# A quantum-attention tower on one core: 82 later weight pieces split during the second layers instead of where they are used

## The reference

```
for t in (er, ei):  h = gelu(ln(x @ W1.T + b1) * g + be)      # first layer,  2048 -> 2048
                    s_t = (h @ W2.T + b2).reshape(tokens, 4, 512)  # second layer, 2048 -> 4*512
q, k, v (real, imaginary) = s_r, s_i times six 512x512 matrices; attention of 4 states, 8 heads
attn_r, attn_i = out @ Wo.T                                   # two more 512x512
R, I   = per state n: attn_r, attn_i times int_Wr[n], int_Wi[n]    # eight 512x512
sup    = sum_ij cos(phase_i - phase_j) * strength_ij * (R_j, I_j), then normalised
amp    = |sup times meas_M (complex)|;  z = gelu(ln(amp @ post_W.T))
y      = relu(relu([z, r_x] @ W_top1) @ W_top2) @ W_top3
```

## Time and profile before

| what | us |
|---|---|
| runs | 3175.32, 3175.93 (median), 3177.78 |
| the profiled execution: its time / its span | 3182.69 / 3181.0 |
| PE busy, DVE busy, ACT busy | 2999.9 (94%), 1573.5 (49%), 1111.3 (35%) |
| first layers, second layers, states (from the span's start) | 0 to 813, 813 to 1597, 1597 to 3181 |
| mean granted clock of PE | 0.979 |

### The profile page before, as it was taken

One profiled execution on the slowest core, in us unless ns is written; L12 is line 12 of the kernel. 1 busy time (PEld: TensorE's weight loads), 2 busy tenths in 40 slices (PEclk: granted clock), 3 DMA queues, 4 the chain that ended last, 5 costly groups with the idle time before them and its releaser, 6 DMA issues. The chain is left out here.

```text
span 3181.0 us, 43948 instructions
## 1 busy us (share of the span) xinstructions
PE 2999.9 (94%) x15808; PEld 2577.4 (81%) x15808; DVE 1573.5 (49%) x2819; ACT 1111.3 (35%) x1873; POOL 232.9 (7%) x241
## 2 busy tenths in 40 slices
PE   7999999999699999999969999999999989999798
PEld 6888888888588877888859999999999977777686
DVE  3222222112531125212156766767757768999973
ACT  3111111111331114211145555555545564555553
POOL 1000000000110011111000000000000000112000
PEclk9999999999899999999989999999999999999899
DMA  5222222121442334332252232232232274444410
GB/s 196 73 76 73 73 75 73 57 65 63 149 143 75 99 96 136 106 99 84 71 185 54 56 90 66 66 86 59 66 92 53 80 189 89 99 88 96 142 41 11
DMA packets 364352, 285.48 MB, mean 90 GB/s; under 512 B 280192, under 2 KB 280320, under 8 KB 364160
## 3 DMA queue, kind: packets, MB, share of 16 engines
q1 hardware_dynamic: 341632, 206.97, 24.3%
q0 software_dynamic: 22656, 77.67, 7.1%
HBM read 194.40 MB, written 90.18 MB: 89 GB/s over the span
## 5 line engine op out<-in xcount | busy, mean ns | idle before, releaser
L50 PE MATMUL banks<-a_whi,a_xhi 128*128 128x512 f32 x1152 | 450.4, 391 | 24.1 <-DVE a_wlo L179 17.6
L51 PE MATMUL banks<-a_wlo,a_xhi 128*128 128x512 f32 x1152 | 449.4, 390 | 0.0
L52 PE MATMUL banks<-a_whi,a_xlo 128*128 128x512 f32 x1152 | 449.3, 390 | 0.0
L50 PE MATMUL banks<-b_ghi,b_whi 128*128 128x512 f32 x1024 | 402.1, 393 | 10.2 <-DVE b_slo L389 8.6
L52 PE MATMUL banks<-b_ghi,b_wlo 128*128 128x512 f32 x1024 | 399.1, 390 | 0.0
L51 PE MATMUL banks<-b_glo,b_whi 128*128 128x512 f32 x1024 | 399.0, 390 | 0.0
L179 DVE TENSOR_TENSOR a_wlo<-a_wraw,a_whi 128x512 fp32r<-128x512 f32 x144 | 99.7, 693 | 577.6 <-ACT a_whi L165 577.6
L165 ACT ACTIVATE a_whi<-a_wraw 128x512 fp32r<-128x512 f32 x144 | 90.9, 631 | 668.1 <-PE banks L52 629.3
L50 PE MATMUL banks<-t_sx,s_whi 128*128 128x256 f32 x1024 | 292.8, 286 | 28.6 <-DVE s_wlo L1267 24.5
L374 DVE TENSOR_TENSOR b_wlo<-b_wraw,b_whi 128x512 fp32r<-128x512 f32 x128 | 88.3, 691 | 444.8 <-ACT b_whi L326 444.6
L52 PE MATMUL banks<-t_sx,s_wlo 128*128 128x256 f32 x1024 | 289.9, 283 | 0.0
(11 more groups left out here) (156 smaller groups left out, 5562.9 us busy)
## 6 DMA issues: line engine op xcount, KB each, us to landing
a_wraw<-w_first SPq DMA_DIRECT2D x144, 256.0 KB, 2.6
b_wraw<-w_second SPq DMA_DIRECT2D x128, 256.0 KB, 2.6
t_sx<-s_scr SPq DMA_DIRECT2D x64, 512.0 KB, 4.5
a_scr<-t_at SPq DMA_DIRECT2D x256, 128.0 KB, 2.1
s_axng<-a_scr SPq DMA_DIRECT2D x64, 512.0 KB, 5.6
s_wraw<-w_pieces SPq DMA_DIRECT2D x82, 256.0 KB, 4.7
h_scr<-a_hst POOLq DMA_DIRECT2D x72, 256.0 KB, 2.7
b_hl<-h_scr POOLq DMA_DIRECT2D x16, 1024.0 KB, 6.0
```

What stands on the lines that cost most here:

```text
L50: mm(out, ahi, bhi, start=first, stop=False)
L51: mm(out, ahi, blo, start=False, stop=False)
L52: return mm(out, alo, bhi, start=False, stop=last)
```

## The change

All 82 pieces are split once, during the second layers, in chunks 1 to 6 of either branch (6 a chunk), chunk 7 of the first (4) and chunk 0 of the second (6): SP loads a piece into `praw`, ACT and DVE split it into `pnew` after the ring's own pieces of steps 3 to 7, SP stores both halves (512 KB) to `w_scr` in DRAM. The split operands of all phases now share two tensors, `g.hi` and `g.lo`. Where the states need weights, SP loads a group of four pieces as two DMAs of 1 MB (hi and lo) straight into places that have died. The first 8 groups are loaded at the end of the second layers: group q once step q of the last chunk has freed its place. `pieces` is gone from ACT and DVE, and PE waits on `w_in[q]` instead of `w_split`.

```diff
+        PRE = 6
+        def prepared(br, c, x):
+            return br * 46 + c * PRE + (x - PRE)
+        def extra(br, c):
+            return 4 if (br, c) == (0, CH - 1) else PRE if (br, c) == (1, 0) else 0
+        AFTER = {3: (0, 1), 4: (2,), 5: (3,), 6: (4,), 7: (5,)}
...
+            def pre_load(p, x):
+                sp.wait_ge(p_split, p + 1)
+                sp.dma_start(praw[:, x % 2, :], g.w_pieces[p]).then_inc(p_loaded[x % 2], 16)
+            def pre_store(p, x):
+                sp.wait_ge(p_split, p + 3)
+                sp.dma_start(g.w_scr[bass.ds(p, 1)].rearrange("o p h w -> p (o h) w"),
+                             pnew[:, x % 2, :, :].bitcast(F32)).then_inc(p_stored[x % 2], 16)
+            def chunk(br, c, n):
                 for j in range(ST):
...
+                    ring(br * CH + c, j)
+                    if j < min(n, 2):
+                        pre_load(prepared(br, c, j), j)
+                    for x in AFTER.get(j - 1, ()) + ((5,) if j == ST - 1 else ()):
+                        if x < n:
+                            pre_store(prepared(br, c, x), x)
+                        if x + 2 < n:
+                            pre_load(prepared(br, c, x + 2), x + 2)
...
+            for q in range(ST):
+                sp.wait_ge(w_used, (2 * CH - 1) * ST + (SPL + q + 1))
+                g.load_pieces(sp, q, q)
...
+            def pre_high(p, x):
+                act.wait_ge(p_loaded[x % 2], (p - x) * 8 + (16 * (x // 2) + 16))
+                act.wait_ge(p_stored[x % 2], (p - x) * 8 + (16 * (x // 2) + 16))
+                act.activation(pnew[:, x % 2, 0, :], praw[:, x % 2, :], ACT.Copy).then_inc(p_hi, 1)
...
                     for j in range(AHEAD, ST):
                         w_high(br * CH + c, j)
+                        for x in AFTER[j]:
+                            pre_high(prepared(br, c, x), x)
...
@@ phase_states, SP @@
             load_s(0, 0)
             load_s(0, 1)
-            for i in range(NP):
-                piece(i)
...
             sp.wait_ge(projected, LAST_B * 8 + 8)
-            for i in range(NP, NP + 2 * KD):
-                piece(i)
+            for q in range(4):
+                g.load_pieces(sp, q, 8 + q)
             sp.wait_ge(v_full, LAST_B * 4 + 4)
             load(0, 0)
+            for q in range(4, 6):
+                g.load_pieces(sp, q, 8 + q)
             store_a(LAST_B - 1)
             load(0, 1)
-            for i in range(NP + 2 * KD, NP + 4 * KD):
-                piece(i)
             store_a(LAST_B)
-            for i in range(NP + 4 * KD, NP + 6 * KD):
-                piece(i)
+            for q in range(6, 8):
+                g.load_pieces(sp, q, 8 + q)
             load(0, 2)
...
             for n in range(3):
                 load(LAST, n)
-            for i in range(2 * NP, 2 * NP + 2 * KD):
-                piece(i)
+            sp.wait_ge(multiplied, LAST * 8 + 2)
+            g.load_pieces(sp, 0, 16)
+            g.load_pieces(sp, 1, 17)
             load(LAST, 3)
...
+        def load_pieces(eng, q, group):
+            n = min(KD, NPIECE - group * KD)
+            for h, to in enumerate((g.hi, g.lo)):
+                eng.dma_start(to[:, q * KD:q * KD + n, :].bitcast(F32),
+                              g.w_scr[group * KD:group * KD + n, :, h, :].rearrange("i p w -> p i w")).then_inc(g.w_in[q], 16)
```

More of the change, by code:

```diff
@@ L245, in phase_second_layers @@
     with s.ctx:
-        ghi = s.sb("ghi", [P, KI, TOK], F32R)
-        glo = s.sb("glo", [P, KI, TOK], F32R)
+        ghi, glo = (t[:, :, :].rearrange("p (k a) w -> p k (a w)", a=2) for t in (g.hi, g.lo))
         wraw = s.sb("wraw", [P, RAW, W])
@@ L262, in phase_second_layers @@
         w_loaded = [s.sem(f"w_loaded{i}") for i in range(RAW)]
+        p_loaded = [s.sem(f"p_loaded{i}") for i in range(2)]
+        p_stored = [s.sem(f"p_stored{i}") for i in range(2)]
+        p_hi = s.sem("p_hi")
+        p_split = s.sem("p_split")
         w_hi = s.sem("w_hi")
@@ L340, in gain_shift @@
                 return g.cols[:, i:i + 1]
+            for i in range(2):
+                act.sem_inc(p_stored[i], 16)
             act.wait_ge(mv_done, 2 * TT)
@@ L423, in _ @@
                                           ALU.subtract).then_inc(g_split, 1)
+                    for x in AFTER.get(j, ()):
+                        if x < extra(br, 0):
+                            pre_low(prepared(br, 0, x), x)
                 for j in range(AHEAD):
@@ L429, in _ @@
                         w_low(br * CH + c, j)
+                        for x in AFTER[j]:
+                            pre_low(prepared(br, c, x), x)
                     for j in range(AHEAD):
@@ L436, in _ @@
                     w_low(br * CH + (CH - 1), j)
+                    for x in AFTER[j]:
+                        if x < extra(br, CH - 1):
+                            pre_low(prepared(br, CH - 1, x), x)
                 s_low(br, CH - 1)
@@ L514, in phase_states @@
     with s.ctx:
[L515 to L519, removed]
+        whi, wlo = g.hi, g.lo
         ids = s.sb("ids", [P, TT, N], mybir.dt.int32)
@@ L830, in _ @@
             sup_back(2)
-            for i in range(2 * NP + 4 * KD, 2 * NP + N_TOP):
-                piece(i)
             store(LAST - 1)
@@ L935, in t_high @@
                                    bias=bcol(M_O + e, m)).then_inc(t_hi, 1)
-            def pieces(i0, i1):
-                for i in range(i0, i1):
-                    act.wait_ge(w_loaded[i % TR], 16 * (i // TR + 1))
-                    act.activation(whi[:, i % NP, :], wraw[:, i % NP, :], ACT.Copy).then_inc(w_hi, 1)
             def block_body(b, first):
@@ L950, in block_body @@
                         o_high(b - 1, m - 1)
-                    if first and m == 1:
-                        pieces(M_V * KD, M_O * KD)
-                    if first and m == 3:
-                        pieces(M_O * KD, NP)
                 if not first:
@@ L1106, in _ @@
             pt_evac(LAST_B, 0)
-            pieces(NP, NP + 2)
             t_high(LAST_B - 1, 2)
@@ L1117, in _ @@
             o_high(LAST_B, 3)
-            pieces(NP + 4, NP + 2 * KD)
             negate(0, 0)
@@ L1262, in t_low @@
                     ins.then_inc(t_split, 1)
-            def pieces(i0, i1):
-                for i in range(i0, i1):
-                    dve.wait_ge(w_hi, i + 1)
-                    dve.tensor_tensor(wlo[:, i % NP, :], wraw[:, i % NP, :], f32(whi[:, i % NP, :]),
-                                      ALU.subtract).then_inc(w_split, 1)
             def block_body(b, first):
@@ L1513, in _ @@
             tile.units()
-            pieces(2 * NP, 2 * NP + 2 * KD)
             sup_low(0)
@@ L1712, in vectors @@
                             w = (2 * n + (x if part == 0 else 1 - x)) * KD + k
-                            if part == 0 and first:
-                                pe.wait_ge(w_split, NP + w + 1)
+                            if part == 0 and first and k == 0:
+                                pe.wait_ge(g.w_in[2 * n + x], 64)
                             a = ax[:, n % 2, :, k, :]
```

84 lines of the change are left out of this document (42 added, 42 removed).

## The result

| kernel | median, us (lowest to highest, executions) | ratio to before, 95% interval |
|---|---|---|
| before, beside it | 3175.62 (3175.15 to 3177.78, 4) | |
| changed | 3214.24 (3211.89 to 3218.88, 4) | 1.0118 [1.0103, 1.0133] |

A forecast was written before the change was run, and what follows sets the result against it. PE, busy 94% of the span, was taken as the bound, with about 40 us at stake at most. -5.9 + 6.8 + 11.3 - 8.3 = +3.9 on a median of 3175.93 gave 3180 us, range 3166 to 3190.

The forecast's parts named there:

- First layers: same instructions at other addresses, 0: First layers: their instructions are unchanged and only tensor addresses move, so 0 us.
- (a): Start of the states: splitting gone, group loads' queue next in line, PE starts at 1615.1 instead of 1621.05; -5.9 us.
- (b): Second layers, second branch's second chunk: late ring piece +4.5, low clock 1.6, h load +0.7; +6.8 us, bounds 0 and +10.
- (c): End of the blocks: block 14's stores queue behind group loads and hold up ACT, then PE; +11.3 us, bounds -2.7 and +17.
- (d): Last stretch: DVE on the path loses 11.1 us of pieces, PE gains part; -8.3 us, bounds -4.9 and -11.1.
- stores not held back: Rival at the end of the blocks: group loads don't delay stores, -2.7 instead of +11.3, 3166 us; chance 0.15.
- second layers hide all: Rival in the second layers: SP's late ring pieces make no stall, 3180 - 6.8 = 3173 us; chance 0.15.
- groups slower than 345 GB/s: Rival, last chunk and end of blocks: group loads slower than the pieces; at 320 GB/s +10.7, 3191 us; chance 0.22.

The follow-up runs named there:

- e1: Kernel before, with only the split x and split activations of the first two stages moved 320 bytes up by unused memory: 3205.31 us, 1.0088.
- e9: Kernel before, with the operands of its last two stages put at multiples of 256 bytes by pads: 3176.31 us, 0.9998.
- e7: Changed kernel, with matmul operands and transfer buffers of every stage at multiples of 256 bytes, no order changed: 3182.91 us, 1.0014.
- e6: e2 with one second-branch piece store issued a chunk later and groups 6 and 7 loaded behind the states' first loads: 3182.40 us, 1.0015.
- e5: e2 with SP's order at the end of the blocks changed, block 14's stores ahead of groups 11 to 13: 3193.88 us, 1.0049.
- e8: e7 with e6's order edits, and stores and tile loads put between the groups at the end of the blocks: 3164.23 us, 0.9959.
- e3: e2 with the last two stages' operands moved 96 or 160 bytes, to the shared halves' remainder by 256: 3194.09 us, 1.0052.
- e4: Kernel before, with e3's shift of the last two stages' operands and nothing of the change: 3180.25 us, 1.0009.
- e2: Changed kernel, with all behind the halves in the first two stages moved 320 bytes up, so both operands have remainder 64: 3191.72 us, 1.0042.
- m1: Kernel before, with rows of split x and split activations 32 bytes longer, so row k stands at remainder 32k by 512: 3210.44 us, one execution.
- m2: Kernel before, with both operands of the first layers stepped by 0 to 96 bytes, all 16 pairs in every chunk: 3195.06 us, one execution.
- e10: Kernel before, with only b_shi and b_slo, sources of the stores into s_scr, 64 bytes higher: 3190.69 us, one execution.

## Why the prediction was wrong

**The step that failed is "First layers: same instructions at other addresses, 0".** It measured +22.3 us there and, by e1, +5.2 to +6.3 in the second layers, 29.1 in all of 38.6. The prediction had seen that the tensors move, wrote the term down and gave it nothing, without a bound and without a rival. The trace before held a hint: matmuls of 128x512 at full clock started 226.7 ns apart in two stages and 231 to 235 in the tiles, and I did not ask why the same form had two rates.

The Trainium skill would not have warned of it: its page "TensorE: Matmul & The Clock Gate", section "Step-by-step: what each phase is for", gives PE two independent read ports, so that loading the next tile's weights takes nothing from the running matmul. The runs agree where the two operands have the same remainder by 256 bytes, and differ by 3% where they don't. That the two reads then meet somewhere is a guess; what happens inside no run shows.

**The other steps, against what they forecast.** The two profiles at multiples of 256, e9 of the kernel before and e7 of the changed one, have equal matmul rates, and their difference is the rest of the change (stages as above, one profile each, us):

| | first layers | second layers and turn | blocks | tiles and top |
|---|---|---|---|---|
| e9 | 837.95 | 781.40 | 965.00 | 589.40 |
| e7 | 837.38 | 789.61 | 975.01 | 579.55 |
| difference | -0.6 | +8.2 | +10.0 | -9.9 |
| forecast | 0 | (a) + (b): +0.9 | (c): +11.3 | (d): -8.3 |

- (a) -5.9 forecast; PE's wait went from 24.4 to 20.9, -3.5 (21.0 in e7). Direction and releaser were as forecast, and the groups moved at 381 GB/s, faster than the 362 taken. The barrier was mis-sized: it came 15.2 us after PE had stopped, 8.5 before, so 6.7 later where 2 to 3 were forecast. POOL's last store, beside groups 6 and 7, landed 11.8 us after issue instead of 5.1, and POOL waited 11.5 us at the meeting of the phases and not 4.84. The states, asked for only then, let PE start 5.7 us later. The row, from the changed kernel:

```profile
1651.71 0.10 POOL L916 MEMSET s_k<- 128x1 f32 x1 [11.51 <-POOLq L244]
```

- (b) +6.8 forecast; the rest of the +8.2 gives about 12, outside its bound of 10. The mechanism was the forecast one (e6). All three terms were undersized. In e7 the wait for the first `slo` is 6.1 us (4.5 forecast), 6.1 us at half clock behind it cost 3.1 (1.6), and the load of h behind the piece loads costs a wait of 1.7 (0.7): its last two took 10.7 and 8.2 us, 6.0 and 6.3 in e9. Half clock behind that wait, in the changed kernel (columns as above):

```profile
1320.30:1323.80 3.50, 3.50 (x8) 2.80 (x9) 3.50 (x6) 2.39 (x5) 2.98 (x3) 0.50 0.34 122
```

- (c) +11.3 forecast, +10.0. ACT waited 18.5 us for the landing of a store, forecast 15 more than the 2.99 of the earlier trace rows. Of these 15.5 us more, PE's two waits show 10.1 (14.6 and 1.4 for 5.91; 12.0 forecast). The step is right and e5 and e8 show its cause.
- (d) -8.3 forecast, -9.9, by a column that moves by some us from profile to profile; the 10.3 became 6.2 (5.4 forecast), and both small waits went, while a new one of 2.0 (3.8 in e7) for `s_ef` from DRAM came.

The sum of the four is +7.8 by these profiles and +5.6 by the medians (e7 against before), where +3.9 was forecast: with the places right, the time would have been 3182.9, 3 us above the forecast. Of the rivals, the first and the third (stores not held back, second layers hide all) are refuted by the 14.6 and the 5.7 us waits; the second (groups slower than 345 GB/s) by 381 (a stretch of the last chunk in the changed kernel):

```profile
1600.00:1635.00 35.00, 35.00 (x155) 28.71 (x153) 3.36 (x6) 3.27 (x5) 0.00 (x0) 1.00 1.03 381
```

Two side sums of the prediction don't come out: at 358 GB/s throughout, (a) would be 1.2 us dearer or more, not 0.9, and groups at 300 GB/s would make (c) +18.5, not +17. Neither bears on the result.

## What to carry to other kernels

A change that moves tensors can be a change of speed. Write down the remainder by 256 bytes of both operands of every matmul of 512 columns before and after, and keep all of a stream's operands at one remainder, best a multiple of 256 (a few unused bytes do it). It pays only where PE sets the pace: e3 and e4 made matmuls faster and gained nothing. When the mean of one unchanged matmul form moves by 1%, count matmuls in a stretch without waits, since that 1% of a duration was 3% of the rate here. Weights prepared early and kept in DRAM pay only if the order of the queue that brings them back is written by need: small stores and loads on which an engine waits go ahead of groups of megabytes.

## What the runs showed of the hardware

- Matmuls of 128x128 by 128x512 in this format start 226.7 ns apart at the full clock in a stream whose stationary and moving operands all have the same remainder by 256 bytes (0 or 64 tried; e2, e7). With a stationary operand at 64 and a moving one at 0 it is about 233.3 (e1), over the map m1 227 to 237, with 192 near the fast value. With the misplaced operand as the moving one it was 228.1 to 230.2. With four operands at different remainders (m2) single passes took 226.6 to 236.3. Those of 256 columns: 120 ns in step, mostly 116 to 125 out of step, no loss.
- A store of 512 KB to `s_scr`, written to DRAM in pieces of 256 bytes through POOL's queue, took 5.4 us from a source at remainder 64 (e10, e2) and 4.0 from one at a multiple of 256 (before, e7). A store of 512 KB to `w_scr`, in runs of 4 KB through SP's queue, took 2.6 us at the fastest whatever the place. The Trainium skill's page "DMA: Bandwidth & Descriptors", section "How a descriptor splits into AXI transactions", says that a descriptor that doesn't start at a multiple of 256 bytes fetches from the boundary below. By its count, an estimate, a run of 4 KB grows from 128 beats to 130, less than 2%, and a piece of 256 bytes from 8 to 10, a quarter. The traces agree in direction: nothing to see with the 4 KB runs, 1.4 us of 4.0 with the pieces. The two stores differ in queue as well, so that the count isn't shown to be the cause.
- Loads of 1 MB from DRAM reached 381 GB/s over 35 us beside a fully busy PE.
- At PE's wait of 5.7 us in the second branch of the changed kernel the granted clock fell to 0.5, the level of 1.2 GHz, for 6.8 us; in e6, where that wait was 1.2 us, it stayed at 1.0.
